# ScalarE makes the first Z chunk of the next pair of n one step earlier in a selective-scan kernel

## The chip, the cores and the metric

One core of one Trainium2 chip runs the whole program. The metric is the device time of one execution in microseconds (us); the lower the better. Engines are called PE (TensorE), ACT (ScalarE), DVE (VectorE), POOL (GpSimd) and SP (SyncE, which here only issues DMAs).

## The reference

The input x is 4 sequences (b) of 512 tokens with 256 channels. The first half is a Mamba-like block, the second a transformer block on the 64 tokens of each sequence that a router chooses. The part that the change touches is the scan over time:

```python
deltaA = jnp.exp(jnp.einsum('bld,dn->lbdn', delta, A))
deltaBu = jnp.einsum('bld,bln->lbdn', delta * u, Bm)
def step(h, inp):
    dA, dBu, c = inp
    h = dA * h + dBu
    return (h, jnp.einsum('bdn,bn->bd', h, c))
```

n runs over 16 states, d over 256 channels. Around it lie a convolution (`cv`), softplus, a gate, an output projection, two layer norms and, after the scan, attention and an MLP over the chosen tokens.

## The kernel before, in words

Each engine has its own instruction list, written out in order by the Python program; the engines meet only in semaphores. The scan is a loop over t from 0 to 63: b is t // 16, and two steps t = 2g and 2g + 1 together do one **pair of n**, g from 0 to 31. A pair needs four **units** u = 4g to 4g + 3 (two per step), each 128 partitions (64 channels times 2 states) by 512 tokens. What is done for them:

- **Z** (`make_z(g, c)`, ACT line 1030): for each of four chunks c of 128 tokens, the rows of delta*u times the column of B of each of the two states, two instructions of 128x256 per chunk. ACT makes chunks 0 to 2, POOL makes chunk 3 (line 1577, in the odd step t for pair t // 2 + 2). `zed` has two slots, so Z of pair g may be written once all four units of pair g - 2 have been transposed (the wait on `bu_filled` in `make_z`, taken at chunk 0). In traces zed is a part of loop_buf.
- **Transposes** (`turn_bu(u)`, PE, helper line 538, bank<-ident,loop_buf): four 128x128 transposes, one per chunk, into one of four PSUM banks. For the first unit of a pair PE waits chunk by chunk for Z, on ACT's count or POOL's.
- **Decay** (`make_decay(u)`, ACT line 1040, front_a<-loop_buf,a_neg): exp of delta times A, 128x512, into a ring of four; decay u waits until unit u - 4 has been scanned.
- **Scan** (`scan(u)`, DVE line 1189): waits for the transposes and the decay of u. The result is called state or copy in traces, by its place.
- **Weigh** (`weigh(t)`, POOL line 1564): the two units of a step times C. **add_states** (PE line 675), three steps later, sums over n.

Beside these, a table (`FRONT_AT`, `TAIL_AT`) puts *pieces* of other work into fixed steps: `fronts(t)` prepare the next b, `tails(t)` finish the last one. On ACT the odd steps hold, relative to the b that is prepared: step 3 of 16 `su`, `r0`, `r1` (with two table loads, lines 938 and 922), step 5 `bc`, step 7 `s1` (lines 971, 972), step 9 `s3` (984), step 13 `du0`, `du1` (902), and of the tails step 5 `o1` and step 15 `ga`, `cs` (1013 to 1017). Even steps hold among others `la0`, `la1` (step 8, ACT line 1007), which scales the rows that DVE's `lx0`, `lx1` (step 9, line 1259, four products of two operands in SBUF) read next. `k0` to `k3` (DVE lines 1272 to 1276) rank the scores from step 11 on; `du1` on PE, which ACT drains at line 902, writes into a PSUM bank that they free.

In each step ACT does, in this order: the two decays for the next step, then (in even steps) Z of pair t // 2 + 1, then tail pieces, then front pieces.

The order of the other engines: PE does in step t unit 2t + 2, add_states(t - 3), tails, unit 2t + 3, fronts. DVE scans 2t and 2t + 1, then tails and fronts. POOL does weigh(t - 1), then in odd steps its Z chunk, then tails and fronts.

Of the kernel before, what the change touches and what calls it, by code (L numbers as in the profile page):

```python
# [91 lines left out]
def block_kernel(nc, x, W_in, conv_w, conv_b, W_x, W_dt, b_dt, A_log, D, W_out, w_router, wq, bq, wk, bk, wv, bv,  # L92
# [6 lines left out]
    C = L // P  # L99
# [42 lines left out]
    T_LAST = B * NST - 1  # L142
    NU = 2 * B * NST

    def tails(t):

        b, n = t // NST, t % NST
        return [(b - 1, piece) for piece in TAIL_AT.get(n, ())] if b >= 1 else []

    def fronts(t):  # L150


        late = {"cv1b": -16, "cv1c": -15, "cv1d": -14}
        return [(b, piece) for b in range(B - 1, 0, -1) for off in sorted(FRONT_AT) for piece in FRONT_AT[off]
                if b * NST + (late.get(piece, off) if b == 1 else off) == t and not (b == 1 and piece in EARLY)]

    def norms(t):

        return NORM_AT.get(t - (B - 1) * NST)
# [48 lines left out]
    with ExitStack() as ctx:  # L208
# [10 lines left out]
        def at(name):  # L219
            return bank[fills.at[name][0]]  # L220
# [10 lines left out]
        def wait_filled(eng, name):  # L231
            i, k = fills.at[name]
            eng.wait_ge(filled[i], k + 1)

        def drain_done(name, ins):
            ins.then_inc(drained[fills.at[name][0]], 1)

        def wait_drained(eng, name):
            i, k = fills.at[name]
            eng.wait_ge(drained[i], k + 1)  # L240
# [650 lines left out]
        def _(act):  # L891
# [102 lines left out]
            def tail(b, piece):  # L994
                name = (piece, b)
                if piece in ("o0", "o1"):
                    o = int(piece[-1])
                    if b >= 1:
                        act.wait_ge(x1_ready, 2 * b)
                        act.wait_ge(chosen_ready, b)  # L1000
                    copy_out(name, flat(z[:, 2 * o:2 * o + 2, :]))
                elif piece in ("la0", "la1"):
                    o = int(piece[-1])
                    act.wait_ge(rstd_ready, 2 * b + o + 1)
                    wait_drained(act, (f"o{o}", b))
                    for c in range(2 * o, 2 * o + 2):
                        ins = act.activation(x1[:, C * b + c, 0:DM], z[:, c, :], ACT.Identity, scale=rstd[:, 0, c:c + 1],
                                             bias=shift[:, 0, c:c + 1])
                    ins.then_inc(rows_ready, 1)
                elif piece == "ga":  # L1010
                    r = K * (b % 2)
                    wait_filled(act, name)
                    drain_done(name, act.activation(sel[r:r + K, b // 2, :], at(name)[r:r + K, 0:NCOL], ACT.Copy))
                elif piece == "cs" and b % 2 == 1:
                    wait_filled(act, name)
                    act.activation(cosT[:, (b // 2) * P:(b // 2 + 1) * P], at(name)[:, 0:P], ACT.Copy)
                    drain_done(name, act.activation(sinT[:, (b // 2) * P:(b // 2 + 1) * P], at(name)[:, P:2 * P], ACT.Copy))

            def make_z(g, c):

                b, m = g // NPAIR, g % NPAIR
                if c == 0:
                    for i in range(2):
                        wait_drained(act, (f"du{i}", b))
                    wait_drained(act, ("cr", b))
                    if g >= NZ:
                        act.wait_ge(bu_filled, 4 * (g - NZ + 1))
                for i in range(2):
                    n = 2 * m + i
                    act.activation(zed[:, g % NZ, c, :, i, :], du_rows[b % 2][:, c, :].rearrange("p (k d) -> p k d", k=2 * KD), ACT.Copy,  # L1030
                                   scale=b_rows[:, b % 2, c, n:n + 1]).then_inc(z_act, 1)

            def make_decay(u):

                b, m, k = u // (2 * NST), u // 4 % NPAIR, u % 4
                if u % (2 * NST) == 0:
                    act.wait_ge(in_delta[b % 2], 16 * 8 * (b // 2 + 1))
                if u >= NDA:
                    act.wait_ge(scanned, u - NDA + 1)
                act.activation(decay[:, u % NDA, :], delta_wide[:, b % 2, k, :], ACT.Exp,  # L1040
                               scale=a_neg[:, k, m:m + 1]).then_inc(decay_made, 1)

            def rows_to_T(name, w):
                p = name[1]
                wait_filled(act, name)
                for k in range(KD):
                    last = act.activation(hT[:, k, p * P:(p + 1) * P], at(name)[:, k * P:(k + 1) * P], ACT.Copy,  # L1047
                                          scale=vec[:, w + k:w + k + 1])
                drain_done(name, last)

            def exchange(p, j):

                name = ("qk", p, j)
                i0 = p * HQK // 2 + j
                wait_filled(act, name)
                if i0 == 0:
                    act.wait_ge(summed, B * NST)
                if i0 >= NQK:
                    act.wait_ge(roped, i0 - NQK + 1)
                mid = HEAD_DIM // 2  # L1060
                src = at(name)[:, 0:2 * P].rearrange("p (a s) -> p a s", a=2)
                act.activation(qk_swap[0:mid, i0 % NQK], src[mid:], ACT.Copy)
                act.activation(qk_swap[mid:, i0 % NQK], src[0:mid], ACT.Copy).then_inc(swapped, 1)

            def copy_v(v):
                if v == 0:
                    wait_filled(act, ("du1", B - 1))
                copy_out(("v", v), v_rows[:, v // 2, (v % 2) * 512:(v % 2 + 1) * 512])
# [34 lines left out]
            make_decay(0)  # L1103
            make_decay(1)
            front(1, "cv0d")
            for t in range(B * NST):
                for u in range(2 * t + 2, min(2 * t + 4, NU)):
                    make_decay(u)
                if t % 2 == 0 and t < T_LAST - 1:
                    for c in range(C - 1):  # L1110
                        make_z(t // 2 + 1, c)
                for b, piece in tails(t):
                    tail(b, piece)
                for b, piece in fronts(t):
                    front(b, piece)
                if norms(t) == "ht":
                    rows_to_T(("h1T", 0), LN1)
            for piece in LAST_TAIL:
                if piece[0] == "q":
                    exchange(0, int(piece[1:]))  # L1120
                elif piece[0] == "v":
                    copy_v(int(piece[1:]))
                else:
                    tail(B - 1, piece)
# [558 lines left out]
```

## Time and profile before

| what | value |
|---|---|
| median of 3 runs | 475.49 us (475.44 to 476.93) |
| the profiled execution | 474.69 us, span 473.0 us |
| mean granted TensorE clock | 0.962 |
| busy over the span: PE, DVE, ACT, POOL | 87%, 63%, 63%, 56% |
| the loop over t | from about 60 us to about 333 us of the span |

The span is from the first to the last instruction on the core. A busy share is an average over stages; a row of a timeline says when a group of instructions began, how long it lasted, how many there were, and in brackets how long the engine had been idle before and what ended that. A "x4" on PE can be two program instructions, since an f32 matmul is recorded as two.

### The profile page before, as it was taken

How to read it: one execution, taken by the hardware profiler on the slowest of the kernel's cores; microseconds unless marked ns; L12 is line 12 of the kernel's file. 1: busy time of each engine (PE TensorE's matmuls, PEld its weight loads, DVE VectorE, ACT ScalarE, POOL GpSimd, SP SyncE). 2: the span in 40 equal slices, each digit the busy share in tenths (PEclk: the TensorE clock that was granted, in tenths of full speed). 3: DMA queues.
4: the chain of work that ended last, by engine and by line, in shares of the span. 5: the costliest groups of instructions: out<-in, count | busy, mean ns of one | idle time of the engine just before them, and what ended most of it. 6: DMA issues, size and time to landing. Idle time of an engine off the chain costs nothing. (4 is left out here: it accounts for less than half of the span.)

```text
span 473.0 us, 6478 instructions
## 1 busy us (share of the span) xinstructions
PE 409.7 (87%) x2037; PEld 248.9 (53%) x2037; DVE 299.8 (63%) x607; ACT 297.4 (63%) x631; POOL 266.7 (56%) x236
## 2 busy tenths in 40 slices
PE   5997899889999989999978789768978999999991
PEld 4442453344446435545434446334765867888880
DVE  0400664469583579865559977999488596554355
ACT  4225689797777697578699586963352565543152
POOL 2001056859688859779776989977553344331022
PEclk9998999999999989999989999978988999999996
DMA  7100611004210002410000515870500000000013
GB/s 238 49 0 21 162 48 43 22 22 116 89 46 22 22 24 51 111 44 22 24 22 14 148 40 165 240 289 1 179 0 2 0 1 1 3 1 0 1 56 122
DMA packets 18709, 29.10 MB, mean 62 GB/s; under 512 B 2698, under 2 KB 10676, under 8 KB 18420
## 3 DMA queue, kind: packets, MB, share of 16 engines
q1 hardware_dynamic: 18676, 28.70, 19.8%
q8 instruction: 16, 0.26, 0.2%
q14 instruction: 17, 0.14, 0.1%
HBM read 22.27 MB, written 2.23 MB: 52 GB/s over the span
## 5 line engine op out<-in xcount | busy, mean ns | idle before, releaser
L1189 DVE TENSOR_TENSOR_SCAN state<-front_a,bank 128x512 f32<-128x512 f32 x88 | 102.7, 1205 | 42.5 <-PE bank L538 21.3
L538 PEld LDWEIGHTS bank<-ident,loop_buf 128*128 128x128 f32 x512 | 59.6, 145 | 84.1 <-issue 34.9
L538 PE MATMUL bank<-ident,loop_buf 128*128 128x128 f32 x512 | 84.8, 288 | 18.2 <-ACT loop_buf L1030 17.7
L1040 ACT ACTIVATE front_a<-loop_buf,a_neg 128x512 f32<-128x512 f32 x128 | 84.1, 712 | 7.2 <-DVE copy L1189 4.6
L1030 ACT ACTIVATE loop_buf<-copy,b_rows 128x256 f32<-128x256 f32 x190 | 79.0, 496 | 0.1
L1564 POOL TENSOR_TENSOR state<-state,front_a 128x1024 f32<-128x1024 f32 x22 | 54.2, 2464 | 21.7 <-DVE state L1189 16.7
L554 PE MATMUL bank<-front_c,conv_raw 128*128 128x512 f32 x128 | 59.2, 594 | 2.5 <-ACT front_c L902 0.9
L1189 DVE TENSOR_TENSOR_SCAN copy<-front_a,bank 128x512 f32<-128x512 f32 x40 | 46.8, 1207 | 20.6 <-ACT front_a L1040 7.7
L1564 POOL TENSOR_TENSOR state<-state,c_own 128x1024 f32<-128x1024 f32 x22 | 52.3, 2380 | 4.4 <-DVE state L1189 4.0
L675 PE MATMUL bank<-state,fold 128*64 128x512 f32 x176 | 50.1, 647 | 0.8 <-POOL state L1564 0.8
L1577 POOL TENSOR_TENSOR loop_buf<-copy,b_rows 128x512 f32<-128x512 f32 x31 | 33.5, 1081 | 28.6 <-ACT copy L902 26.0
L554 PEld LDWEIGHTS bank<-front_c,conv_raw 128*128 128x128 f32 x128 | 22.5, 191 | 22.3 <-issue 20.3
L1593 POOL TENSOR_TENSOR loop_buf<-state 128x256 f32<-128x256 f32 x24 | 17.8, 743 | 27.0 <-DVE state L1341 27.0
L1564 POOL TENSOR_TENSOR copy<-copy,front_a 128x1024 f32<-128x1024 f32 x10 | 25.5, 2548 | 7.4 <-DVE copy L1189 7.4
L1545 POOL TENSOR_TENSOR copy<-front_c,front_b 128x1024 f32<-128x1024 f32 x4 | 8.0, 2000 | 37.4 <-ACT front_b L902 32.4
L902 ACT ACTIVATE front_b<-bank,vec 128x512 f32<-128x512 f32 x16 | 10.9, 682 | 26.8 <-PE bank L554 23.7
L902 ACT ACTIVATE copy<-bank 128x512 f32<-128x512 f32 x20 | 11.7, 595 | 23.3 <-PE bank L538 13.2
L1564 POOL TENSOR_TENSOR copy<-copy,c_own 128x1024 f32<-128x1024 f32 x10 | 24.0, 2405 | 2.9 <-DVE copy L1189 2.6
L699 PE MATMUL bank<-h,copy 128*128 128x128 f32 x192 | 24.2, 281 | 1.4 <-ACT h L1047 0.9
L699 PEld LDWEIGHTS bank<-h,copy 128*128 128x128 f32 x192 | 22.8, 194 | 4.3 <-issue 3.0
L675 PE MATMUL bank<-copy,fold 128*64 128x512 f32 x80 | 22.5, 641 | 0.0
L1207 DVE TENSOR_SCALAR front_c<-front_b 128x512 f32<-128x512 f32 x2 | 0.9, 428 | 30.4 <-ACT front_b L966 30.4
(201 smaller groups left out, 726.5 us busy)
## 6 DMA issues: line engine op xcount, KB each, us to landing
front_a<-c_stage SPq DMA_DIRECT2D x32, 128.0 KB, 2.9
c_own<-c_stage SPq DMA_DIRECT2D x32, 128.0 KB, 2.9
loop_buf<-front_b SPq DMA_DIRECT2D x32, 128.0 KB, 2.3
copy<-in_L_attn_x SPq DMA_DIRECT2D x4, 512.0 KB, 3.7
front_b<-in_L_ffn_wo SPq DMA_DIRECT2D x1, 2048.0 KB, 10.0
copy<-in_L_ffn_wq SPq DMA_DIRECT2D x1, 2048.0 KB, 8.1
out<-loop_buf SPq DMA_DIRECT2D x3, 512.0 KB, 3.0
conv_raw<-in_L_attn_conv_w SPq DMA_DIRECT2D x2, 512.0 KB, 3.8
```

Of the source, the lines that this page charges most:

```text
L538: return pe.transpose(dst, src, ident[:])
L554: mm = pe.matmul(at(name)[:], conv_x[:, k, i, o * P:(o + 1) * P], xT[:, i, k:k + L], start=(j == 0), stop=(j == TAPS * KD - 1))
L675: mm = pe.matmul(bank[Y_BANK[h]][j * P // 2:(j + 1) * P // 2, :], fold[:], state[t % NH][:, j, :], start=(m == 0), stop=(m == NPAIR - 1))
L699: mm = pe.matmul(at(name)[:, i * P:(i + 1) * P], w_qk[:, k, head * P:(head + 1) * P], hT[:, k, p * P:(p + 1) * P], start=(k == 0), stop=(k ...
L902: drain_done(name, act.activation(dst, at(name)[:] if src is None else src, func, **kw))
L1030: act.activation(zed[:, g % NZ, c, :, i, :], du_rows[b % 2][:, c, :].rearrange("p (k d) -> p k d", k=2 * KD), ACT.Copy, scale=b_rows[:, b ...
L1040: act.activation(decay[:, u % NDA, :], delta_wide[:, b % 2, k, :], ACT.Exp, scale=a_neg[:, k, m:m + 1]).then_inc(decay_made, 1)
L1189: dve.tensor_tensor_scan(state[t % NH][:, j, :], decay[:, u % NDA, :], bank[BU_BANK[u % NBU]][:], 0.0, ALU.mult, ALU.add).then_inc(scanned, 1)
L1545: pool.tensor_tensor(resT[b % 2], xT[:, :, PAD:], xsT, ALU.add).then_inc(res_ready, 1)
L1564: pool.tensor_tensor(state[t % NH], state[t % NH], c_wide[g % NCW].unsqueeze(1).to_broadcast([P, 2, L]), ALU.mult).then_inc(weighed, 1)
L1577: pool.tensor_tensor(zed[:, g % NZ, c], rows, cols, ALU.mult).then_inc(z_pool, 1)
L1593: pool.tensor_tensor(qkT[:, 2 * j:2 * j + 2, p * P:(p + 1) * P], qk_raw[:, i0 % NQK], qk_swap[:, i0 % NQK], ALU.add).then_inc(roped, 1)
```

## The change

The loop over steps on ACT makes chunk 0 of Z at the end of each odd step, for the pair whose chunks 1 and 2 follow in the next even step. The even step made all three. The first such chunk, of pair 1, stands ahead of the loop. Nothing else is edited: PE, DVE, POOL and SP keep their instructions and their order, and the number and the size of ACT's instructions are the same.

```diff
             front(1, "cv0d")
+            make_z(1, 0)
             for t in range(B * NST):
                 for u in range(2 * t + 2, min(2 * t + 4, NU)):
                     make_decay(u)
                 if t % 2 == 0 and t < T_LAST - 1:
-                    for c in range(C - 1):
+                    for c in range(1, C - 1):
                         make_z(t // 2 + 1, c)
                 for b, piece in tails(t):
                     tail(b, piece)
@@
                 if norms(t) == "ht":
                     rows_to_T(("h1T", 0), LN1)
+                if t % 2 and t < T_LAST - 2:
+                    make_z(t // 2 + 2, 0)
```

On ACT, at the end of step 39 and the start of step 40 (piece `s1` is L971 and L972, `la0` and `la1` are L1007; L1040 are decays, L1030 Z). The same piece stands at steps 23 and 24:

```order
 L971 ACTIVATE front_b<-front_b 128x1024
 L972 ACTIVATE front_b<-front_b 128x1024
-L1040 ACTIVATE front_a<-loop_buf,a_neg 128x512 x2
-L1030 ACTIVATE loop_buf<-copy,b_rows 128x4x64 x6
+L1030 ACTIVATE loop_buf<-copy,b_rows 128x4x64 x2
+L1040 ACTIVATE front_a<-loop_buf,a_neg 128x512 x2
+L1030 ACTIVATE loop_buf<-copy,b_rows 128x4x64 x4
 L1007 ACTIVATE x<-z,shift,rstd 128x256 x4
```

The two instructions of chunk 0 have moved ahead of the two decays of step 40; what follows the last Z instruction stands where it stood.

On ACT, at the end of step 19 and the start of step 20 (`r0` and `r1` are L902 copy, with the second table load behind them):

```order
 L902 ACTIVATE copy<-bank 128x512 x2
 L922 ACT_TABLE_LOAD
-L1040 ACTIVATE front_a<-loop_buf,a_neg 128x512 x2
-L1030 ACTIVATE loop_buf<-copy,b_rows 128x4x64 x6
+L1030 ACTIVATE loop_buf<-copy,b_rows 128x4x64 x2
+L1040 ACTIVATE front_a<-loop_buf,a_neg 128x512 x2
+L1030 ACTIVATE loop_buf<-copy,b_rows 128x4x64 x4
 L902 ACTIVATE z<-bank 128x512
```

Here too chunk 0 goes between the odd step's last piece and the even step's decays.

## Rows read from the trace of the kernel before

**Rows 1.** The page, part 5: decays and Z on ACT: busy, mean ns.

```profile
L1040 ACT ACTIVATE front_a<-loop_buf,a_neg 128x512 f32<-128x512 f32 x128 | 84.1, 712 | 7.2 <-DVE copy L1189 4.6
L1030 ACT ACTIVATE loop_buf<-copy,b_rows 128x256 f32<-128x256 f32 x190 | 79.0, 496 | 0.1
```

**Rows 2.** Waits of PE: engine, line, releaser: us in total, times, longest.

```profile
PE bank L538 <- ACT loop_buf L1030: 17.7, 32, 2.2
```

**Rows 3.** Timeline, steps 39 to 41, all engines: start, us, instruction, idle before.

```profile
241.30 1.32 ACT L1040 ACTIVATE front_a<-loop_buf,a_neg 128x512 f32<-128x512 f32 x2
242.10 2.33 DVE L1189 TENSOR_TENSOR_SCAN copy<-front_a,bank 128x512 f32<-128x512 f32 x2 [0.99 <-PE bank L538]
242.53 2.49 ACT L1030 ACTIVATE loop_buf<-copy,b_rows 128x256 f32<-128x256 f32 x6
...
243.56 1.03 POOL L1577 TENSOR_TENSOR loop_buf<-copy,b_rows 128x512 f32<-128x512 f32 x1
243.56 0.30 PE L538 MATMUL bank<-ident,loop_buf 128*128 128x128 f32 x1 [2.21 <-ACT loop_buf L1030]
...
244.27 0.33 PE L538 MATMUL bank<-ident,loop_buf 128*128 128x128 f32 x1 [0.41 <-ACT loop_buf L1030]
244.56 2.36 POOL L1564 TENSOR_TENSOR copy<-copy,front_a 128x1024 f32<-128x1024 f32 x1
...
245.07 0.44 PE L538 MATMUL bank<-ident,loop_buf 128*128 128x128 f32 x2 [0.47 <-ACT loop_buf L1030]
...
246.04 1.17 DVE L1259 CUSTOM_DVE_ANT_0 junk<-x,router 128x256 bf16<-128x256 f32 x1 [1.61 <-ACT x L1007]
...
247.48 0.42 DVE L1259 CUSTOM_DVE_ANT_0 junk<-x,router 128x256 bf16<-128x256 f32 x1
...
248.17 1.22 DVE L1221 SCALAR_TENSOR_TENSOR front_b<-front_c,front_b 128x1024 f32<-128x1024 f32 x1
...
251.77 3.19 POOL L1564 TENSOR_TENSOR state<-state,front_a 128x1024 f32<-128x1024 f32 x1 [4.86 <-PE bank L538]
```

**Rows 4.** Chain that ended last, 240 to 266 us: start, us, what.

```profile
263.61 0.04 issue
263.65 0.67 PE bank L538 x4
...
264.35 0.60 ACT copy L902
```

**Rows 5.** Windows: length, busy us (instructions) of PE, PEld, DVE, ACT, POOL; granted clock; DMA.

```profile
171.20:175.90 4.70, 4.70 (x14) 2.00 (x14) 3.42 (x10) 4.70 (x9) 1.32 (x1) 0.69 0.00 0
...
244.00:248.50 4.50, 3.76 (x14) 1.95 (x15) 2.89 (x10) 4.50 (x9) 2.92 (x2) 0.69 0.00 0
246.10:263.60 17.50, 13.22 (x68) 6.82 (x64) 17.50 (x40) 14.39 (x27) 12.51 (x7) 0.91 0.21 45
```

**Rows 6.** Timeline, steps 23 to 25, DVE and POOL.

```profile
167.70 2.33 DVE L1189 TENSOR_TENSOR_SCAN state<-front_a,bank 128x512 f32<-128x512 f32 x2 [0.99 <-PE bank L538]
...
170.17 2.35 POOL L1564 TENSOR_TENSOR state<-state,front_a 128x1024 f32<-128x1024 f32 x1
...
171.64 1.17 DVE L1259 CUSTOM_DVE_ANT_0 junk<-x,router 128x256 bf16<-128x256 f32 x1 [1.60 <-ACT x L1007]
...
174.70 1.23 DVE L1221 SCALAR_TENSOR_TENSOR front_b<-front_c,front_b 128x1024 f32<-128x1024 f32 x1 [0.84 <-ACT front_c L975]
```

**Rows 7.** Timeline of DVE: step 7, then steps 20 and 22.

```profile
97.57 2.33 DVE L1189 TENSOR_TENSOR_SCAN state<-front_a,bank 128x512 f32<-128x512 f32 x2 [0.99 <-PE bank L538]
102.59 1.23 DVE L1221 SCALAR_TENSOR_TENSOR front_b<-front_c,front_b 128x1024 f32<-128x1024 f32 x1 [2.69 <-ACT front_c L975]
...
147.16 1.22 DVE L1189 TENSOR_TENSOR_SCAN state<-front_a,bank 128x512 f32<-128x512 f32 x1 [4.40 <-issue]
149.07 1.22 DVE L1189 TENSOR_TENSOR_SCAN state<-front_a,bank 128x512 f32<-128x512 f32 x1 [0.69 <-PE bank L538]
152.09 1.22 DVE L1189 TENSOR_TENSOR_SCAN copy<-front_a,bank 128x512 f32<-128x512 f32 x1 [1.79 <-ACT front_a L1040]
```

## The prediction

> **What bounds the kernel now.** I read the page, then the waits of PE, then the chain that ended last, then the timeline of all engines where the chain and the change meet. No engine bounds the whole loop: the chain goes back and forth between ACT, PE and DVE. What the change aims at is PE waiting for ACT's Z, 17.7 us in 32 waits [rows 2]. The reader is to see which of a pair's chunks PE waits for. At 243.56 it waits 2.21 us for chunk 0, transposes it, waits 0.41 us for chunk 1, then 0.47 us for chunk 2, and does chunks 2 and 3 in 0.44 us [rows 3]. A transpose is short against the two Z instructions of a chunk (six last 2.49 us, so two 0.8 us [rows 3]; 496 ns each in the page [rows 1], overlapping a little). So the unit is complete 0.44 us after ACT's last Z instruction, whenever chunk 0 came. All that PE does next is queued behind that.
>
> **The change, part by part.**
>
> *ACT's own sum: 0.* 190 Z instructions and 128 decays before and after [rows 1], none added. At a pair, before: two decays 1.23 us (241.30 to 242.53), six Z instructions 2.49 us, end at 245.0 [rows 3]. After: two Z 0.8, two decays 1.2, four Z 1.65; the same end. What stands behind it on ACT (`la0` here) starts when it did.
>
> *PE's wait for Z: 0.* Chunk 0 is ready about 1.2 us earlier (the two decays), the last chunk at the same time. The 2.21 us at 243.56 would become about 1.0, and the next wait 1.2 longer. The last chunk could come earlier only where ACT waits between the odd step's pieces and the last Z, that is for the scan that frees a decay buffer. ACT waits before decays for 7.2 us in all [rows 1], nearly all of it around 314 to 324 us of the span, where DVE has no gap; I cost that at 0 too. From below it could be worth up to the whole 17.7 us [rows 2], from above 0; I take 0, since the row of the third wait is the nearest.
>
> *The moved chunk's wait for its slot: 0.* At step 39's end it needs the transposes of the pair two before, which PE finished before it took up the units of the next pair; PE is already waiting for this very Z at 243.56 with those behind it [rows 3].
>
> *The decays of the even step come 0.8 us later.* This is the only thing that arrives late. Behind them stand DVE's scans, then POOL's weigh, then PE's add_states three steps on. In ten places of the loop DVE is waiting for just that decay: its scan starts within 0.12 us of the end of the first decay. They are the even steps behind a step with `su` and the table loads, `bc`, `s1` or `du1`, at 80.33, 88.56, 97.57, 122.71, 147.16, 158.69, 167.70, 221.55, 233.09 and 242.10 us; some are put down to PE or "issue" in the brackets, but the decay ends nearest (241.30 plus 0.71 is 242.01, scan at 242.10 [rows 1, 3]; the first of the ten that is shown is 97.57, and 147.16 is a table-load one [rows 7]). In the steps without such a piece the decays run ahead of DVE. So the bounds are 0 and 10 times 0.8, 8 us.
>
> Which of the ten pass it on? DVE is idle again soon after each, mostly for more than 0.8 us: 2.69 us at 102.59 [rows 7], and at 147.16 0.69 us before the second scan and then 1.79 more [rows 7]. Nine are absorbed on DVE so. PE needs the bank of a scanned unit only four units later, and POOL's weigh feeds an add three steps later. Cost of these nine: 0.
>
> The tenth is step 40, at 242.10. DVE itself is idle 1.61 us afterwards, until `lx0` at 246.04, so the scans absorb. POOL does not. Its weigh starts at 244.56, when its Z chunk is done and 0.13 us after the scans end (242.10 plus 2.33 is 244.43) [rows 3]. With the scans 0.8 later they end at 245.23, weigh starts about 245.25 and ends 2.36 later, at 247.6 instead of 246.92. And the first product of `lx0` cannot run beside it: it took 1.17 us and ended 0.3 us after weigh's end, where the next ones take 0.42 us [rows 3]. It would end near 247.9 instead of 247.2: **+0.7 us** on DVE. From 246.1 to 263.6 DVE has no gap (17.50 busy of 17.50 [rows 5]), `k0` to `k3` end it, and PE's transposes for `du1` wait for the bank they free; ACT drains these at 264.35, and all of that is the chain [rows 4]. POOL's next weigh, at 251.77, follows DVE too [rows 3]. Behind 264 us the chain runs through ACT, PE and DVE to the end, and I find nothing that would take the 0.7 us back.
>
> The Trainium skill, "SBUF — State Buffer", section "Who interferes with whom", says that a Vector instruction with two SBUF inputs and a GpSimd instruction that reads SBUF exclude each other, for the whole instruction, whoever came first holding on. That rule speaks against the change, and the trace agrees: 1.17 us against 0.42 us.
>
> The same order stands in step 24, and there it is absorbed: weigh at 170.17 would shift by about 0.6 and the first product with it (it ran 171.64 to 172.8), but DVE stood idle 0.84 us before the next instruction at 174.70 [rows 6]. At step 8 no `lx` follows.
>
> *Sum:* 0 + 0 + 0 + 0.7. The profiled execution took 474.69 us for a span of 473.0, 0.8 under the median of 475.49; so 475.4 profiled, and 475.49 + 0.7 = **476.2 us** as a median. That is +0.15%; about 0.3%, 1.4 us, is what a measurement of this kernel can tell from no change, so the forecast counts as no change.
>
> **The rivals.**
>
> *All absorbed (0.25): 475.5 us.* The gapless DVE stretch may have slack that a busy row hides, or `la0` may decide: then +0.7 does not reach 263.6. For it: nine of ten places absorb. Against it: the window has no idle time at all.
>
> *The clock holds, faster (0.10): 474.0 or 472.6 us.* After the waits for Z at 243.56 and the like at step 25, the granted clock is 0.69 on average in 171.2 to 175.9 and in 244.0 to 248.5 [rows 5], so partly the lower of the levels 1.2 and 2.4 GHz; PE had transposed little and waited before both. The part lost is 4.7 times 0.31, 1.5 us, and 4.5 times 0.31, 1.4 us. Chunk 0's transpose now falls into the middle of the wait. If that kept the clock up and PE decided there, one place gives 474.0, both 472.6. Against it: PE's total idle time stays, one transpose is 0.3 us, and DVE decides from 246 on. The Trainium skill, "TensorE: Matmul & The Clock Gate", section "What's actually happening", says that activity releases the throttle and idleness brings it back, which would favour this rival; the trace shows the fall behind idle time but not whether one transpose prevents it.
>
> *The late decays decide at `s1` in every b, slower (0.20): 477.7 us.* Place: steps 8, 24 and 40. Price: 0.7 to 0.8 us each, three of them 2.2. It decides from the point where ACT's `s2` and the copies before it no longer end later than DVE's queue: in step 25 that is a delay over 0.84 us [rows 6], near the 0.6 that I worked out; and in step 8 a gap of 2.69 us [rows 7] must be used up. I hold it less likely for that last one.
>
> **How the numbers follow.** Forecast 0.45, all absorbed 0.25, faster 0.10, slower 0.20. The predicted time is the first's, 476.2. The range, 474.4 to 477.9, holds the forecast, the absorbed case, the slower case at its price and the top of the clock case; what it leaves out is most of the clock case and the tail in which more of the ten places pass their 0.8 us on. Within 0.3% are the first two and small parts of the others, 0.73; faster 0.09 and slower 0.18.
>
> **What would show it.** PE's wait for line 1030 stays between 16 and 19 us, with a longer second wait in each pair. ACT's busy time and its last Z of a pair stay in place relative to the pieces. DVE waits 0.8 us longer before the scans of steps 4, 6, 8, 14, 20, 22, 24, 36, 38 and 40. The first `lx0` product near 246 us takes about 1.9 us instead of 1.17, and everything from there is 0.7 us later; up to 242 us the two timelines agree within 0.2 us. I am wrong if Z's last chunk ends earlier against the pieces before it, if the clock rows at 171 and 244 read near 1.0, or if PE's add_states begin to wait for weigh.

## The result and the profile after

The changed kernel took **479.09 us** (median of 20 runs, 475.51 to 485.84), the kernel before 475.51 us (20 runs, 472.32 to 480.89). The ratio is 1.0061, with a 95% interval of 1.0034 to 1.0087: slower by 0.6%. (Ratios here leave out executions more than 1.5% above the fastest of their kernel, so this is not the quotient of the two medians, 1.0075.) The forecast was 476.2 us and no change, the range ended at 477.9. It was wrong.

The executions of one kernel scatter widely here, and how they scatter belongs to the answer: of 183 executions of the kernel before, in all batches of this study, 49 (27%) took over 478.5 us; of 32 of the changed one 20 did.

The profiled execution of the changed kernel took 485.84 us (span 483.1, mean granted clock 0.942), so it is the costliest of its 20, beside one of before of 474.69 us (span 473.0, clock 0.962). What it shows as a place and a cause can be read; its total can't be set against the median.

What ACT and PE do in all. The page, part 5, and PE's waits:

```profile
L1040 ACT ACTIVATE front_a<-loop_buf,a_neg 128x512 f32<-128x512 f32 x128 | 85.1, 710 | 6.9 <-DVE copy L1192 3.8
L1030 ACT ACTIVATE loop_buf<-copy,b_rows 128x256 f32<-128x256 f32 x190 | 82.0, 496 | 0.4
```

```profile
PE bank L538 <- ACT loop_buf L1030: 17.7, 23, 1.6
```

ACT's instructions last what they did [rows 1]; PE's wait for Z is 17.7 us as before, in 23 pieces where there were 32 [rows 2]. The piece of program of [rows 3], after the change (timeline of all engines):

```profile
248.83 0.89 ACT L1030 ACTIVATE loop_buf<-copy,b_rows 128x256 f32<-128x256 f32 x2
249.63 1.32 ACT L1040 ACTIVATE front_a<-loop_buf,a_neg 128x512 f32<-128x512 f32 x2
249.87 0.30 PE L538 MATMUL bank<-ident,loop_buf 128*128 128x128 f32 x1 [0.98 <-ACT loop_buf L1030]
250.43 2.33 DVE L1192 TENSOR_TENSOR_SCAN copy<-front_a,bank 128x512 f32<-128x512 f32 x2 [1.79 <-issue]
250.85 1.69 ACT L1030 ACTIVATE loop_buf<-copy,b_rows 128x256 f32<-128x256 f32 x4
...
251.80 0.33 PE L538 MATMUL bank<-ident,loop_buf 128*128 128x128 f32 x1 [1.63 <-ACT loop_buf L1030]
...
252.60 0.69 PE L538 MATMUL bank<-ident,loop_buf 128*128 128x128 f32 x2 [0.47 <-ACT loop_buf L1030]
252.83 2.36 POOL L1567 TENSOR_TENSOR copy<-copy,front_a 128x1024 f32<-128x1024 f32 x1 [0.70 <-DVE copy L1192]
...
253.56 1.92 DVE L1262 CUSTOM_DVE_ANT_0 junk<-x,router 128x256 bf16<-128x256 f32 x1 [0.81 <-ACT x L1007]
```

This is the predicted picture. Chunk 0 stands ahead of the decays, PE's first wait is 0.98 us instead of 2.21 and the second 1.63 instead of 0.41, Z ends where it did, the scans start 1.79 us after DVE's last work instead of 0.99 (0.8 late), weigh 0.7 late behind them, and the first `lx0` product takes 1.92 us instead of 1.17. The bracket at DVE says "issue", which is why the prediction went by the decay's end: 249.63 + 0.71 is 250.34, and the scan starts at 250.43.

Where the time went is in windows whose borders are the starts of DVE's scans of steps 0, 10, 14, 27, 32, 41, 47, 51 and 63. (The prediction counted by ACT's steps: the late decays of ACT's step 40 are DVE's step 41.) Before; the columns are those of [rows 5], the clock is the number ahead of the last two:

```profile
60.30:103.70 43.40, 38.09 (x165) 18.40 (x164) 24.48 (x21) 38.20 (x70) 30.61 (x16) 1.00 0.09 28
103.70:117.30 13.60, 13.53 (x59) 6.05 (x58) 13.19 (x12) 10.79 (x23) 10.91 (x4) 1.00 0.37 83
117.30:179.20 61.90, 56.80 (x261) 29.60 (x262) 38.02 (x47) 49.41 (x92) 45.27 (x32) 0.97 0.13 43
179.20:200.20 21.00, 20.31 (x95) 10.43 (x94) 19.26 (x38) 13.96 (x28) 18.46 (x9) 1.00 0.34 87
200.20:242.10 41.90, 39.29 (x183) 20.32 (x180) 24.29 (x30) 31.70 (x58) 34.03 (x27) 1.00 0.10 29
242.10:269.20 27.10, 19.49 (x102) 10.46 (x104) 25.32 (x49) 23.24 (x47) 21.89 (x12) 0.94 0.25 63
269.20:282.40 13.20, 12.06 (x70) 6.79 (x66) 10.55 (x11) 9.54 (x22) 11.37 (x6) 1.00 0.14 49
282.40:329.10 46.70, 36.98 (x196) 21.01 (x196) 42.99 (x71) 31.49 (x63) 39.77 (x30) 0.91 0.54 181
```

The same stretches of the changed kernel:

```profile
61.00:106.40 45.40, 39.90 (x163) 19.10 (x162) 24.98 (x22) 38.58 (x70) 30.59 (x16) 0.92 0.08 28
106.40:122.30 15.90, 15.90 (x62) 7.00 (x61) 14.79 (x12) 10.43 (x22) 9.85 (x4) 0.91 0.40 99
122.30:184.40 62.10, 55.87 (x248) 28.48 (x248) 38.66 (x47) 49.53 (x92) 45.35 (x32) 0.95 0.10 35
184.40:207.80 23.40, 22.71 (x111) 12.04 (x108) 18.24 (x39) 14.07 (x28) 18.51 (x10) 1.00 0.31 79
207.80:250.40 42.60, 39.34 (x183) 20.43 (x181) 24.12 (x29) 32.46 (x60) 34.77 (x27) 1.00 0.10 32
250.40:277.50 27.10, 21.21 (x96) 11.72 (x97) 26.10 (x49) 22.41 (x44) 21.20 (x12) 0.79 0.24 59
277.50:292.60 15.10, 13.70 (x75) 7.75 (x73) 10.68 (x12) 9.79 (x23) 11.30 (x6) 0.92 0.12 39
292.60:339.20 46.60, 36.61 (x196) 21.00 (x196) 42.89 (x71) 31.33 (x63) 39.74 (x30) 0.91 0.54 181
```

The lengths change by 2.0, 2.3, 0.2, 2.4, 0.7, 0, 1.9 and -0.1 us, 9.4 together; 0.7 more lies ahead of the loop, and the spans differ by 10.1. Three things are to be seen.

- **0.7 us in the fifth row** is the late scan at its end, and the sixth row, as long as before, does not give it back: the forecast's one cost.
- **2.0, 2.3, 2.4 and 1.9 us** lie where PE ran partly at 1.2 instead of 2.4 GHz, or had just done so: the clock was 0.50 from 177.4 to 184.2 us, just ahead of the fourth row, in which PE does 111 instructions where it did 95 and so catches up on what was left at the border. In the first two rows the clock took 8% of 45.4 us and 9% of 15.9 us, 5.1 us of PE's work at full clock, and they are 4.3 us longer: in the second PE is busy for 13.53 of 13.60 us before, so it decides.
- **0 us in the sixth row**, though the clock was 0.79 on average, 5.7 us of PE's work under full clock and 4.1 more than before. Its first low stretches cost nothing: the scans of steps 42 to 48 all stand 7.6 us later than before, and DVE, from the `lx0` product on, has no gap. Its last one is paid in the seventh row: the clock was 0.50 from 273.1 to 279.9 us, across the border at 277.5, and PE does 96 instructions where it did 102, then 75 where it did 70. So the same lower clock costs nothing where DVE is ahead of PE, and nearly all of it where PE is busy from end to end.

So the trace names two causes: the lock on the port that DVE and POOL share, and the granted clock. The first was foreseen, the second costs more. Whether the change makes the clock worse, or the profiled execution only met it, one trace can't tell.

### The profile page after: what moved, and what is told of

It reads as the page before. It is cut to its first block and busy times, and to the rows that moved or that the text cites. A ratio compares the mean times of both kernels' runs of the same rounds, so it can differ in the third digit from the quotient of the medians.

```text
span 483.1 us, 6478 instructions
## 1 busy us (share of the span) xinstructions
PE 417.9 (87%) x2037; PEld 253.4 (52%) x2037; DVE 302.1 (63%) x607; ACT 297.9 (62%) x631; POOL 265.9 (55%) x236
## 5 line engine op out<-in xcount | busy, mean ns | idle before, releaser
L538 PEld LDWEIGHTS bank<-ident,loop_buf 128*128 128x128 f32 x512 | 61.7, 149 | 84.1 <-issue 42.4
L538 PE MATMUL bank<-ident,loop_buf 128*128 128x128 f32 x512 | 85.6, 295 | 18.2 <-ACT loop_buf L1030 17.7
L1040 ACT ACTIVATE front_a<-loop_buf,a_neg 128x512 f32<-128x512 f32 x128 | 85.1, 710 | 6.9 <-DVE copy L1192 3.8
L1030 ACT ACTIVATE loop_buf<-copy,b_rows 128x256 f32<-128x256 f32 x190 | 82.0, 496 | 0.4
L554 PE MATMUL bank<-front_c,conv_raw 128*128 128x512 f32 x128 | 62.5, 622 | 3.3 <-ACT front_c L902 1.7
L675 PE MATMUL bank<-state,fold 128*64 128x512 f32 x176 | 52.7, 678 | 0.8 <-POOL state L1567 0.8
L1580 POOL TENSOR_TENSOR loop_buf<-copy,b_rows 128x512 f32<-128x512 f32 x31 | 32.5, 1049 | 30.2 <-ACT copy L902 26.8
L902 ACT ACTIVATE front_b<-bank,vec 128x512 f32<-128x512 f32 x16 | 10.9, 683 | 31.8 <-PE bank L554 28.7
L902 ACT ACTIVATE copy<-bank 128x512 f32<-128x512 f32 x20 | 11.7, 595 | 24.0 <-PE bank L538 13.9
```

Source lines behind the costliest of these rows:

```text
L538: return pe.transpose(dst, src, ident[:])
L554: mm = pe.matmul(at(name)[:], conv_x[:, k, i, o * P:(o + 1) * P], xT[:, i, k:k + L], start=(j == 0), stop=(j == TAPS * KD - 1))
L675: mm = pe.matmul(bank[Y_BANK[h]][j * P // 2:(j + 1) * P // 2, :], fold[:], state[t % NH][:, j, :], start=(m == 0), stop=(m == NPAIR - 1))
L902: drain_done(name, act.activation(dst, at(name)[:] if src is None else src, func, **kw))
L1580: pool.tensor_tensor(zed[:, g % NZ, c], rows, cols, ALU.mult).then_inc(z_pool, 1)
```

## The experiments

Each was timed in five rounds beside the kernel before on the same chip. "Above" is the number of its executions over 478.5 us; the clock is the mean over executions (one of 512.93 us left out; of the kernel before, over the 163 of the experiments' batches). "Above" is not a count of falls of the clock: the profiled executions of e10 (477.72 us) and e12 (477.39 us) had two costly ones and lie below the line. And a kernel that is 0.8 us slower by itself crosses the line more easily: 57 of the 183 executions of before (31%) are over 477.7 us.

| kernel | median us | ratio to before (95%) | clock | above |
|---|---|---|---|---|
| before, all batches | 475.5 to 477.3 | | 0.956 | 49 of 183 |
| the change (first batch) | 479.09 | 1.0061 (1.0034 to 1.0087) | 0.950 | 11 of 20 |
| e1 before again | 476.21 | 0.9993 (0.9955 to 1.003) | 0.952 | 4 of 12 |
| e2 the change again | 479.68 | 1.0071 (1.0035 to 1.0106) | 0.949 | 9 of 12 |
| e3 all pairs but 21 | 479.79 | 1.0060 (1.0021 to 1.0099) | 0.956 | 8 of 12 |
| e4 pair 21 alone | 478.81 | 1.0035 (0.9998 to 1.0072) | 0.956 | 7 of 12 |
| e5 before, Z waits filled | 475.22 | 1.0006 (0.9976 to 1.0036) | 0.967 | 0 of 12 |
| e6 change, Z waits filled | 477.31 | 1.0039 (1.0003 to 1.0075) | 0.963 | 3 of 12 |
| e7 before, PE waits for chunk 1 | 475.52 | 1.0002 (0.9964 to 1.0039) | 0.959 | 1 of 12 |
| e8 change, chunk 0 held on PE | 477.70 | 1.0046 (1.0015 to 1.0077) | 0.956 | 2 of 12 |
| e9 all but 21, Z waits filled | 476.19 | 0.9969 (0.9923 to 1.0015) | 0.968 | 2 of 12 |
| e10 quiet pairs alone | 478.99 | 1.0069 (1.0026 to 1.0112) | 0.954 | 7 of 12 |
| e11 waiting pairs alone | 475.12 | 0.9989 (0.9950 to 1.0028) | 0.959 | 1 of 12 |
| e12 all but 21, held | 477.19 | 1.0050 (1.0011 to 1.0090) | 0.953 | 5 of 12 |
| e13 before, all waits filled | 475.94 | 0.9944 (0.9908 to 0.9981) | 0.983 | 0 of 12 |
| e14 change, all waits filled | 476.73 | 0.9983 (0.9945 to 1.0020) | 0.983 | 2 of 12 |
| e15 all but 21, all filled | 475.05 | 0.9933 (0.9899 to 0.9966) | 0.986 | 0 of 12 |
| e16 quiet pairs, all filled | 475.24 | 0.9955 (0.9925 to 0.9986) | 0.984 | 0 of 12 |
| e17 = e10 again | 479.29 | 1.0036 (0.9994 to 1.0079) | 0.954 | 7 of 12 |
| e18 = e11 again | 477.15 | 1.0008 (0.9967 to 1.0049) | 0.954 | 4 of 12 |

Medians of different batches differ by up to 1.8 us for the very same kernel before, so compare ratios across batches, and times inside one: e1 to e4, e5 to e8, e9 to e12, e13 to e16, e17 and e18.

### The lock: all pairs but 21, and pair 21 alone

The chunks that move are chosen by pair:

```diff
+            moved = [g for g in range(1, B * NPAIR) if g != 21]      # e4: g == 21
...
-                    for c in range(1, C - 1):
+                    for c in range(1 if t // 2 + 1 in moved else 0, C - 1):
...
-                if t % 2 and t < T_LAST - 2:
+                if t % 2 and t < T_LAST - 2 and t // 2 + 2 in moved:
```

e1 (before again) and e2 (the change again) gave the batch its two ends. What was expected of the four, in this order, each text with its theories:

> The kernel before, unchanged, against itself: how its times and its clock scatter. Both theories: ratio 1.000. Theory L (lock: at step 40 the later scans push weigh into lx0, +0.7 us) says nothing of it. Theory C (clock: the rest of the 2.9 us is PE's granted clock, because chunk 0's transpose has left the idle time and made it emptier): the mean clock of the executions lies about 0.960, and an execution is about 1.2 us longer for each stretch at the lower clock within the loop.

> The change as it is, measured beside the others. Ratio about 1.006. Theory C: mean clock about 0.951, lower than the kernel before by about 0.008, with more stretches at the lower clock between 60 and 300 us of the span. Rival (theory L alone, the rest being scatter of the first measurement): ratio 1.0015, and the mean clock is the same within 0.002.

> The change for all pairs but pair 21 (step 39's end). Theory L: 0.7 us faster than the full change, and the first lx0 product near 246 us takes 1.17 us again, followed by no shift. Theory C: the clock stays as low as with the full change, ratio about 1.0045. If L were all of it: ratio 1.000.

> The change for pair 21 alone. Theory L: the timeline agrees with the kernel before up to 242 us, then DVE is 0.7 us later and stays so to the end: ratio 1.0015. Theory C: the clock as with the kernel before within 0.002, so the same ratio; the full 1.006 here would mean that one place makes it all.

The change is slower again, by 0.7%. e1's profiled execution took 512.93 us at a mean clock of 0.821 (span 510.7 us, 38 us over before's) and is left out. With pair 21 left alone (e3), the lock is gone. Timeline of DVE, ACT and POOL behind its step 40:

```profile
247.07 2.33 DVE L1194 TENSOR_TENSOR_SCAN copy<-front_a,bank 128x512 f32<-128x512 f32 x2 [0.99 <-PE bank L538]
...
249.54 2.37 POOL L1569 TENSOR_TENSOR copy<-copy,front_a 128x1024 f32<-128x1024 f32 x1
251.01 1.17 DVE L1264 CUSTOM_DVE_ANT_0 junk<-x,router 128x256 bf16<-128x256 f32 x1 [1.61 <-ACT x L1007]
```

Product 1.17 us, wait 0.99, as before [rows 3]; e4 has 1.92 us and 1.78, and its window from the scan of step 32 to that of 41 is 42.70 us long, e3's 41.90. Yet e3 lost as much as the change, and e4 half of it (its interval still holds 1). So the lock is real and is not the main cost.

### PE's waits for Z: filled, merged, held

Theory C said that moving chunk 0 empties PE's idle stretch, so that the clock falls more often; theory D that ACT's order costs by itself. Four kernels. e5 and e6 put transposes of the identity, whose result the next real transpose overwrites, into the waits for Z of nine pairs, so many ahead of each chunk, in e5 of before, in e6 of the change (there 5 to 12 of them ahead of chunk 1 in place of those ahead of chunk 0; pair 21 keeps 7 there too). The edit of e5:

```diff
+            FILL = {3: (4, 3, 3, 0), 5: (9, 3, 3, 0), 10: (0, 3, 3, 0), 13: (9, 3, 3, 0), 18: (0, 3, 3, 0),
+                    21: (16, 3, 3, 0), 22: (4, 3, 3, 0), 25: (0, 3, 3, 0), 28: (2, 3, 3, 0)}
...
                     if k == 0:
+                        for _ in range(FILL.get(g, (0, 0, 0, 0))[c]):
+                            turn(bank[BU_BANK[u % NBU]][:, c * P:(c + 1) * P], ident[:])
```

e7 is the kernel before with PE waiting for chunk 1 ahead of chunk 0, e8 the change with PE's chunk 0 held until the even step's second decay is done:

```diff
-                            pe.wait_ge(z_act, z_count(g, c))
+                            pe.wait_ge(z_act, z_count(g, 1 if g and c == 0 else c))      # e7
...
                             pe.wait_ge(z_act, z_count(g, c))
+                            if g and c == 0:                                             # e8
+                                pe.wait_ge(decay_made, 4 * g)
```

> The kernel before, with transposes of the identity added on PE while it waits for Z of pairs 3, 5, 10, 13, 18, 21, 22, 25 and 28 (2 to 22 per pair, 0.11 us each at full clock, into the bank that the unit fills anyway). Theory C (the clock: PE's idle pieces before the chunks decide how often the granted clock falls, and a stretch at 1.2 GHz costs 1 to 2.5 us where PE decides): fewer low stretches between 60 and 333 us, mean clock over 0.962, time 472 to 475 us. Theory D (the order on ACT itself delays work, the clock only follows): the same time as before, 475 to 477 us, or slower where a filler is late.

> The changed kernel with such transposes in its own waits for Z, most of them between chunk 0 and chunk 1. Theory C: the clock comes back as in the filled kernel before, and only POOL's lock at step 40 stays: within 1 us of the filled kernel before, 472.5 to 476 us. Theory D: 478.5 to 480.5 us as the changed kernel, 3 us over the filled kernel before.

> The kernel before, its ACT order untouched; only PE waits for chunk 1 of Z before it transposes chunk 0, so that its idle time before a pair's first unit is one piece of up to 2.7 us in place of two. The unit is complete as before. Theory C: the clock falls more often, as with the change: 477.5 to 480 us, mean clock 0.950. Theory D: 475.5 to 476.5 us.

> The changed kernel, its ACT order untouched; only PE transposes chunk 0 not before the even step's second decay is done, which is when it could do so in the kernel before. PE's idle pieces are then those of before. Theory C: mean clock back to 0.956 to 0.960 and the time at 475.9 plus the lock's 0.7, 476 to 477.3 us. Theory D: 479 to 480 us, since the decays are as late as with the change.

e7's wait for Z is now 19.5 us in 25 pieces, the longest 3.0, and it is not slower: one long gap in place of two is not the cause, and theory C in that form fell. e8's waits are cut where before's are (PE waits, total, times, longest):

```profile
PE bank L538 <- ACT loop_buf L1032: 10.1, 23, 0.5
...
PE bank L538 <- ACT front_a L1042: 6.8, 7, 2.2
```

It took 477.70 us, between C's 476 to 477.3 and D's 479 to 480, and is still clear of before (1.0046, 1.0015 to 1.0077). Filling raised the clock from 0.957, before's in this batch, to 0.967 in e5 and bought nothing there. The change filled stayed 2.1 us over before filled, where C said 1 and D said 3. Inconclusive, except for e7.

### Which pairs: quiet, waiting, held

> Chunk 0 moved for every pair but 21 (so without POOL's lock at step 40), with the filling transposes in PE's waits for Z. Theory C (chunk 0's transpose leaves PE's idle stretch, the granted clock falls more often for it; filled up, that can't be): as the filled kernel before, 475.2 us, 474.5 to 476, mean clock 0.966. Theory D (the late decays cost time by themselves): 477.5 to 479 us, as all but 21 had without filling.

> Chunk 0 moved for the 22 pairs before which PE does not wait for it or for chunk 1 in the kernel before; left for pairs 3, 5, 10, 13, 18, 21, 22, 25 and 28. Theory C: nothing happens, since no transpose moves in time on PE: 475.5 to 476.2 us, mean clock 0.957. Theory D: a part of the loss, by the number of pairs two thirds of it: 477.5 us.

> Chunk 0 moved only for eight pairs before which PE waits for it or for chunk 1: 3, 5, 10, 13, 18, 22, 25 and 28. Theory C: the loss of all but 21 in full, 478.5 to 479.8 us, mean clock 0.950 to 0.955. Theory D: a third of it, 476.5 us.

> Chunk 0 moved for every pair but 21, but PE transposes it only once the even step's second decay is done, as in the kernel before; neither the lock nor the shift on PE is left. Theory C: the time of before, 475.5 to 476.2 us, mean clock 0.957. Theory D: 479 us, since ACT's order is that of all but 21.

The lists of `moved` and the held wait are the edits shown above. e12 shares e8's surplus (1.0050, 1.0011 to 1.0090) with no lock in it, which C didn't allow for. e10 and e11 came out the wrong way round: the pairs before which PE doesn't wait carried the loss, those before which it waits carried none. But look at the profiled execution of e10, the first two windows and the seventh:

```profile
58.80:102.20 43.40, 38.09 (x162) 18.24 (x161) 24.50 (x22) 38.20 (x70) 30.56 (x16) 0.96 0.10 28
102.20:118.40 16.20, 16.20 (x63) 7.36 (x63) 14.63 (x12) 10.73 (x22) 9.87 (x4) 0.91 0.40 98
...
270.30:285.30 15.00, 13.85 (x75) 7.83 (x74) 10.55 (x11) 9.74 (x23) 11.34 (x6) 0.93 0.11 36
```

The profiled execution of e11 (480.81 us), the waiting pairs, met costly falls too; its first two windows:

```profile
60.40:105.80 45.40, 39.89 (x163) 19.00 (x162) 24.96 (x21) 38.56 (x70) 30.58 (x16) 0.92 0.08 28
105.80:121.80 16.00, 16.00 (x62) 7.06 (x61) 14.85 (x12) 10.53 (x22) 9.88 (x4) 0.91 0.42 97
```

e10's second window is 16.20 us instead of 13.60. The clock fell at 98.4 us, and up to 99 us every PE instruction of the loop starts, counted from the first scan, within 0.03 us of where it does in before. The same work on the same schedule fell there in one execution and not in another (e4 fell there too, 16.20 us). The Trainium skill, "TensorE: Matmul & The Clock Gate", section "What's actually happening", says that the gate's own time base does not restart with a kernel and that where its changes land varies from run to run; the traces agree.

### All of PE's long waits filled

To take the clock out altogether, e13 to e16 fill, beside Z (now of fourteen pairs), PE's waits for `u` (first `dt`), `dt` (`dl0`), the bank of `du1`, `x1` (`sb`) and `chosen` (`pf`):

```diff
+            def keep(dst, n):
+                for _ in range(n):
+                    turn(dst, ident[:])
...
+                if name == ("du1", 3):
+                    pe.wait_ge(scanned, 2 * 45 + 1)
+                    keep(bank[BU_BANK[(2 * 45 + 4) % NBU]][:, 0:P], 13)
                 wait_free(pe, name)
...
+                    if b == 2:
+                        keep(t[:, 0:P], 14)
                     pe.wait_ge(chosen_ready, b + 1)
```

> The kernel before, with transposes of the identity in all of PE's waits of over 0.4 us from the first dt to the prefix sums of b = 2: for Z, for u and dt, for the bank of du1, for x1 and for chosen. Theory C (the clock): hardly a low stretch between 60 and 333 us, mean clock over 0.970, no runs at 479 to 482 us, median 472 to 474.5 us. Theory D (ACT's order costs by itself): the same kernel, since the order is that of before.

> The changed kernel with the same filling. Theory C: over the filled kernel before by the lock at step 40 alone, 0.7 us: 472.7 to 475.2 us. Theory D: 2.5 to 3.5 us over it.

> Chunk 0 moved for all pairs but 21, with the same filling. Theory C: the filled kernel before, within 0.5 us. Theory D: 2 to 3 us over it.

> Chunk 0 moved for the 22 quiet pairs alone, with the same filling. Theory C: the filled kernel before, within 0.5 us. Theory D: 2 to 3 us over it, as without filling.

This settled the first half. The windows of e13 (before, filled), rows one, two, four, five, six and seven:

```profile
60.20:103.60 43.40, 41.47 (x197) 21.66 (x196) 24.49 (x22) 38.19 (x70) 30.58 (x16) 1.00 0.09 28
103.60:117.20 13.60, 13.53 (x59) 6.06 (x58) 13.16 (x13) 10.79 (x22) 10.91 (x4) 1.00 0.37 81
...
179.10:199.90 20.80, 20.11 (x94) 10.23 (x93) 19.26 (x39) 13.93 (x28) 18.46 (x10) 1.00 0.34 91
199.90:241.70 41.80, 41.20 (x202) 22.44 (x201) 24.22 (x29) 31.66 (x58) 33.94 (x27) 1.00 0.08 28
241.70:269.00 27.30, 23.22 (x152) 14.49 (x151) 25.49 (x50) 23.42 (x47) 22.09 (x12) 1.00 0.25 65
269.00:282.40 13.40, 13.02 (x80) 7.77 (x79) 10.51 (x12) 9.45 (x22) 11.29 (x6) 1.00 0.14 46
```

And of e14 (the change, filled), without the fourth, which is 20.80 us too:

```profile
60.40:104.30 43.90, 41.94 (x199) 22.00 (x198) 24.96 (x21) 38.62 (x70) 30.61 (x16) 1.00 0.09 29
104.30:117.50 13.20, 13.13 (x58) 5.94 (x57) 13.11 (x13) 10.39 (x22) 10.54 (x4) 1.00 0.36 81
...
200.40:243.10 42.70, 42.01 (x210) 23.18 (x208) 24.18 (x30) 32.51 (x60) 34.89 (x27) 1.00 0.09 32
243.10:270.20 27.10, 22.57 (x148) 14.20 (x148) 26.12 (x49) 22.41 (x44) 21.21 (x12) 1.00 0.24 60
270.20:283.60 13.40, 13.04 (x81) 7.98 (x81) 10.72 (x12) 9.75 (x23) 11.37 (x6) 1.00 0.14 43
```

At full clock the change lengthens the fifth row by 0.9 us, where all but 21 filled (e15) has 41.80 as before filled. Beside it stand only 0.2 us more in the third row and 0.2 less in the sixth; 0.5 in the first is back but for 0.1 in the second. Over all eight rows before filled is 268.9 us, the change filled 269.9, all but 21 filled 269.0. In medians 475.94, 476.73, 475.05 and 475.24 (quiet pairs): D's 2 to 3 us are not there in any of the three. The 0.8 us between the first two medians would prove little alone (their ratios, 0.9944 with 0.9908 to 0.9981 and 0.9983 with 0.9945 to 1.0020, overlap); the rows show where it is. **At full clock ACT's new order costs 0.8 to 1.0 us, nearly all by the lock; the rest of the 3.6 us between the first batch's medians is there only when the clock is left to fall.**

Two more things stand here. e13's rows are as long as before's though its clock is 1.00: before's profiled execution met its low stretches only where they cost next to nothing (0.2 us, 21.00 against 20.80 in the fourth row). And the filled kernels' slowest executions end at 476.3 to 478.7 us, where before goes up to 484.

### The pair repeated

> The quiet pairs alone, once more. Theory E (the quiet pairs make the clock fall): 478.5 to 479.5 us again, over half of the executions above 478.5 us. Theory C (the waiting pairs do): 475.5 to 476.5 us. Theory L (a dozen executions are too few: the share that meets costly low stretches scatters from kernel to kernel): 476 to 478 us, a third above 478.5.

> The eight waiting pairs alone, once more. Theory E: 475 to 475.7 us, hardly an execution above 478.5 us. Theory C: 478 to 479.5 us. Theory L: 476 to 478 us, a third above 478.5.

Quiet: 479.29 again, seven of twelve above. Waiting: 477.15, four of twelve. Over both batches quiet has 14 of 24 (mean 478.9 us) and waiting 5 of 24 (mean 476.2), with before at 27% (mean 476.8). In these two texts L is no longer the lock but chance, a dozen executions being too few. L's third above does not fit the quiet pairs, E's "hardly one" not the waiting ones. Yet the profiled execution of e17 took 476.21 us, and its second window was 13.60 us long, as before's, in the same program as e10's 16.20.

## Why the prediction was wrong

*ACT's sum 0, and PE's wait for Z 0*: right. The wait is 17.7 us before and after; with chunk 0 held back (e8) it is 10.1 and 6.8.

*Decays 0.8 us late in ten places, nine absorbed*: right. In the change, e6, e8 and e14 the scans of DVE's steps 5, 7, 9, 15, 21, 23, 25, 37, 39 and 41 start 0.8 us later against those around them, and all but the last give it back. Of the nine, 0.4 us remains between steps 10 and 14 and 0.2 from step 16 on. Against the kernel before the 0.2 seems gone by 32, but that one had lost 0.2 itself to a low clock; against before filled, all but 21 filled keeps 0.2 up to step 48 and 0.1 to the end. So the slower rival (the late decays decide at `s1` in every b) gave nothing; its time, 477.7, was the nearest for the wrong reason.

*The lock, +0.7*: right in kind, place and size: 1.92 us against 1.17 for the product where 1.9 was said, 0.8 us that stays in e4 and is missing in e3, 0.8 between the medians of e13 and e14, and 0.9 between the fifth rows of e14 and e15. As the Trainium skill, "SBUF — State Buffer", section "Who interferes with whom", would have it, a DVE instruction with two SBUF inputs waits out a POOL one that reads SBUF and came first: the product ends 0.3 us behind weigh's end (255.48 and 255.19).

*The clock*: **this is the step that failed.** The sum had no term for it, and the only rival that named it let it change in one direction, up, and priced it at 1.5 and 1.4 us in the two places where the profiled execution had it low. Both are wrong. Those two places cost next to nothing: filled, they show a clock of 1.00 and rows of the same lengths but for 0.2 us. The costly places, behind 98 us and behind 265 us, (times of the kernel before) showed 1.00 in that execution, and PE's 13.53 busy us of 13.60 behind the first, a stretch of which the prediction says nothing, said that a fall there costs what it takes. One execution was taken for the kernel: 474.69 us is one of its cheap ones, and the median carries a share that isn't in it. In the changed kernel 20 of 32 executions lie above 478.5 us, where before has 27% (31% above 477.7, which allows for the lock); that is about 3 us in the median (3.6 less 0.8, and 3.8 less 0.8 in e2's batch). The prediction's own sign failed by it as well: up to 242 us the two timelines were to agree within 0.2 us, and the change's scan of step 40 stands 6.9 us late (e14's, against e13, 0.3).

**What stays open** is by which of the moved chunks. Three readings disagree. Holding chunk 0 back on PE alone brings the share above 478.5 us from 28 of 44 (the change and e3) to 7 of 24 (e8 and e12), which speaks for PE's emptied idle stretch; both profiled executions of the unfilled change fell behind pair 13's wait, in steps 25 and 26, for so long (177.4 to 184.2 us in the first) that the steps from 27 to 32 took 2.3 us longer. But e8 and e12 are still 0.5% slower than before, and falls at that very place stand in the traces of before (clock 0.51 from 170.6 to 174.0 us), e7, e8, e17 and e18 too, half as long and costing 0.1 to 0.6 us. But the waiting pairs alone have no excess, and the quiet ones alone have it, with no PE instruction moved ahead of the fall that cost most. The kept traces show that no choice of pairs is needed for the fall that starts about 40 us behind the first scan: those of the change, e2, e3, e4, e10, e11 and e12 have it, those of before, e7, e8, e17 and e18 have not, and e10 and e17 are one program, e11 and e18 another. With a dozen executions a kernel and a spread of 2.5 us among them, the pairs can't be told apart, and I don't settle on one.

## What to carry to other kernels

When the mean granted clock of a profile is below 1 and some stretch has PE busy from end to end, ask what the clock does there in the other executions: read the spread of all executions first, and take one profile for one draw. An edit that should be neutral can still shift how often the costly draws come; the way to tell its own cost from that is to fill PE's waits in both kernels with transposes nobody reads, and compare those. And of a step that is moved ahead of others, the neighbours that it makes late are priced one by one: nine of ten gave their 0.8 us back, and the tenth was kept by a weigh of POOL that a product of DVE had to wait out.

The filling may also be worth having for itself: before filled is 0.56% faster than before by the ratio (0.9944, 0.9908 to 0.9981), all but 21 filled 0.67% (0.9933, 0.9899 to 0.9966), which can't be told apart. That rests on one batch, in which before had the highest of its six medians, 477.26 us; the quotient of e13's median and this one is 0.9972, and in the other five batches before has 475.5 to 475.9 us, no more than e13's 475.94. What it gains comes from cutting the longest executions, not by a better best case (471.5 us against 472.2).

## What was unexpected of the hardware

- The same program on the same schedule is granted 1.00 or 0.91 in the same stretch, from one execution to the next (13.60 or 16.20 us, e17 and e10); behind 98 us that decides 2.6 us.
- The mean clock of an execution does not tell its time: e10 has executions of 476.65 and 479.02 us at a mean clock of 0.962, where before has 472.2 to 478.3 us. It is the place that counts.
- Filling the waits for Z raised the clock by 0.010 in before (0.957 in its batch to 0.967) and left the median as it was (ratio 1.0006); filling all long waits raised it by 0.03, to 0.983, at a ratio of 0.9944.
